# A four-layer graph network kernel: VectorE's own semaphore instructions replaced by waits for tile releases, with a new order of the steps

## The chip, the cores and the metric

The kernel runs on one core of a Trainium2 chip. Its time is the device time of one execution in microseconds (us), the median of three runs. A core has five engines with queues of their own: TensorE (PE), VectorE (DVE), ScalarE (ACT), GpSimd (POOL) and SyncE (SP, which issues the DMAs). They meet only through semaphores.

## The reference

`x` is 32 batches of 512 nodes with 128 features, `adj` one 512x512 adjacency matrix of ones and zeros. Four graph layers follow each other, each on the normalised input and added to it:

```python
h = jnp.maximum(_layernorm(x, axis=-1), 0.0)
x = x + _L0_gnn_ref(h, adj, ...)   # attention with pair indices, softmax over rows, plus h @ self_weight
h = jnp.maximum(_layernorm(x, axis=-1), 0.0)
x = x + _L1_gnn_ref(h, adj, ...)   # attention, layernorm, aggregation, two-layer MLP
h = jnp.maximum(_layernorm(x, axis=-1), 0.0)
x = x + _L2_gnn_ref(h, adj, ...)   # attention, elu
h = jnp.maximum(_layernorm(x, axis=-1), 0.0)
x = x + _L3_gnn_ref(h, adj, ...)   # out = softmaxed edge weights: diagonal @ h0 + rest @ h1 + bias
```

Layers 1 and 2 hold the attention that matters here: `e = leaky_relu(s_i + t_j)`, masked by `adj`, softmax over j, times the features.

## The kernel before, in words

The 32 batches are worked in 16 groups of two. A group has 1024 rows, which lie as 8 tiles of 128 rows by 128 features in SBUF. Six groups are under way at a time, each in a slot `s` with its own buffers (`X[s]` the residual, `Y[s]`, `HE[s]`, `HT[s]` the transposed rows, `HI[s]`/`LOW[s]` a value split in two parts, `CE[s]`, `MX[s]` small coefficients); so group 13 is in slot 1, groups 14 and 15 in slots 2 and 3, group 11 in slot 5.

A group passes through 56 steps, listed in `STEPS` with the engines that take part. The suffix is the layer. For layers 1 and 2: `stat` (DVE's `bn_stats`, POOL's reciprocal root), `scale` (ACT writes the normalised rows), `norm` (PE transposes them, ACT copies with relu), `feat` (features times weights; DVE copies two score columns out and takes their maximum), `top` (PE spreads the maximum, DVE makes exponents, ACT takes the exponentials), `weigh`, `spreada`/`spreadb` (PE spreads one score per batch over a tile), `atta`/`attb` (DVE makes the attention matrix `PT`, four instructions of 128x512, L1307; PE multiplies it with the features, 16 matmuls), then `collect`/`gat`/`gin`/`mlp` in layer 1 and `elu2a`, `elu2b`, `elu2` in layer 2. Layer 0 has `coef0`, `cmax0`, `coefb0` (narrow matmuls of 4 columns, `wcols` and `CS`), `split0`, `agg0`, `self0`; layer 3 has `feat3` (`W3`, 256 columns) and `agg3` (48 matmuls on `a3_hi` and `a3_lo`). `PREP` is a seventeenth list, work done once on the edge weights.

The order in which an engine takes the steps is written out by hand: in `TURNS`, one digit per step says from which group (0 to 9, a to f; g is `PREP`) the next step comes. Each engine has its string, and within a group the steps keep their order. Nothing is decided at run time: an engine whose next step is not ready stands still.

PSUM is cut into 8 banks of 128x512. `HOMES` gives the bank of each tile in PE's order. Each bank has two semaphores, `psum_full` (PE has written) and `psum_taken` (the reader has read; PE may write again). PE asks with `turned(...)` or `open_tile(...)`, a reader asks with `filled(...)` and raises `taken` on its last instruction. `read_by_act(...)` on DVE waits for a tile's release, here that of DVE's own instruction, and so until DVE has finished it. Only two `PT` buffers exist (`RING`).

The steps that the change touches, on DVE: `split0` (L1227 on) scales a tile pair twice, into `YF` and `VA`; `attend` (L1296 on) makes `PT`; `elud2` (L1345 on) is `elu2a` and `elu2b`; `agg3` (L1466 on) adds the last result to `X`. At the end of each DVE waits until it has finished and then raises a semaphore with an instruction of its own:

```python
a.then_inc(p_full[r], 1)
dve.wait_ge(p_full[r], u.matrix(name)[1] + 1)
dve.sem_inc(read, 1)
```

That is the end of `attend`. Of the raises, `scaled` is waited for by ACT's `split0`, `read` (the release of the spread tile) by PE's later tile in that bank, `gated` by ACT's `elu2` and `result` by SP's `store`.

Of the kernel before, what the change touches and what calls it, by code (L numbers as in the profile page):

```python
# [41 lines left out]
RING = 2  # L42
# [78 lines left out]
    "pe": ("gggg0110101020g2120012413240303410101033114040511522553305120232123223032304143130550100001110404151"  # L121
           "4214515042454505252101321322624224226736676743472662373343234433643474684867688646786758757383757785"
           "84838848854595599599655a6a99a56a6a79799699669769657a56656a777787a78776b6ab8abb8aa67b78aab8b889798ba8"
           "bacb8cbb8c9b9dadadbc8c89dd9899ca9aaaca99ade9aecaccdeeccbcedbdcdeedb9dbdde9e9bebeebbcbecefbfffafbbcdf"
           "cfdaafffdffdfcfccceccdecddcfdfeddedffbdeeefefeffebeecffdcffbdcedfefef"),
    "act": ("g0110g2021g01244303011200341105501103015142021303221023021351033012001014114250542403105245402215314"
           "512243563222446372573644622372343473346443688668747668537537655638847748854788599755596aa9686a659798"
           "76699a76956765957997776a87ab866b6788baa77878baaa889ab9b8caac9bbd98ada8cbb898d9cab99a9adaabeeccc9cbed"
           "dcabe9cddbbce9ded9bcbeebbbcdfecfaedfacfcbdedaffdfdfcceffcdcecdeffecfdfdedffbbeedffeeefffbcdcedfcdefe"
           "fef"),  # L130
    "dve": ("g102gggg1010g0g0204131120001112234504032110330411041520352201313355422022331330045241134555000101200"
           "2414001145151412553042230451615422372242262627667633446652737673233434834764438677866484388674785788"
           "6736585783884987455799a9595956a99a98566a55799a99a6866775966a596aa77b667787767ab7ab988a6abbbc7ba8bb8a"
           "a7988bdab8cb8b889d9caabdcc8d9dc89bca9eacd9cad9aa9becca9ddce9ceeebddceeeddbabd9cae9ecbebfebdcffbffdbb"
           "fbefccffadeaffffddebcfcccefcfcdcdfdededffcddeedffeebeeffeffefcfddcbefef"),
    "pool": ("01201043120153240135234010521430510021421562374626234736847783865384547989a596a96755a679ab67687b87bc"
           "ab98da89c8adbcae9cdde9ebc9ebdabfcfafefdcdfcebfdefcdbecfdefef"),
    "sp": ("403510617228394a5b6c7d8e9fadcbef"),
}
HOMES = ("0123456701234567012347056123412341235641702356415670415067125304304356717204356072071241207431256074"  # L140
         "3612543612354072361546150723461341634613461507234615072346150723461613450726712345016273473273250164"
         "7324732432473501647235021364721364507213607452136260745264051372640513762517640325031725031371250303"
         "0643071625642565307615423073067306713540276540465270413040410310652743103146527652703140314652703146"
         "5270314652462574031640235702135647021356024756024756060612437506750567124376105246105246371052463716"
         "3710524367105721045367210721074503764076354542154207163546356435643543207165436543652407316247357325"
# [20 lines left out]
def gnn_kernel(nc, x, adj, Wo_d, Ws_d, att0_d, Wp_d, bp_d, asrc_d, adst_d, gatg_d, gatb_d, eps_d, W1_d, b1_d,  # L166
# [12 lines left out]
    with ctx:  # L179
# [74 lines left out]
        class Step:  # L254
# [18 lines left out]
            def matrix(self, name):  # L273

                m = mat_at[name, self.group]
                before = mat_of[m - RING] if m >= RING else None
                return m % RING, m // RING, before
# [382 lines left out]
        with nc.Block() as block:  # L660
# [483 lines left out]
            def _(dve):  # L1144
# [200 lines left out]
                def elud2(u, s, b):  # L1345
# [14 lines left out]
                    for h in range(2):  # L1360
                        read_by_act(u, "att2" + "ab"[b], s, h)
# [163 lines left out]
```

## Time and profile before

| | us |
|---|---|
| median of three runs | 1015.85 |
| lowest and highest run | 1012.22, 1019.29 |
| profiled execution, span from first to last instruction | 1013.8 |
| PE busy | 949.6 |
| DVE busy | 859.2 |
| ACT busy | 632.5 |
| POOL busy | 555.4 |

The page gives no other time of the profiled execution than its span. Busy is the time in which at least one instruction of the engine runs. Matmuls overlap each other, and their ends are modelled. Waits and instructions that only raise a semaphore are not counted as busy. "Idle before <- X" names who released the instruction that the engine waited with.

### The profile page before, as it was taken

Reading aid. Unit: us, or ns where it says so; the run is one execution under the profiler, and the core shown is the slowest. Engines: PE = TensorE matmul, PEld = TensorE weight load, DVE = VectorE, ACT = ScalarE, POOL = GpSimd, SP = SyncE. Lnnn points to the kernel's source line nnn. Section 1 sums busy time; section 2 is a strip of 40 time slices with the busy share of each in tenths; the row PEclk is TensorE's granted clock in tenths of the full one; section 3 lists DMA queues with packets and bytes.
Section 4 is the critical chain, followed back from the end, with each engine's and each line's share of the span. In section 5 each row is a group of like instructions: output and inputs, shape, how many; then the busy total and the mean of one; then the engine's idle time right before and its main releaser. Section 6 shows DMA issues by size and latency. Waiting matters only on the chain. (4 is left out here: it accounts for less than half of the span.)

```text
span 1013.8 us, 21212 instructions
## 1 busy us (share of the span) xinstructions
PE 949.6 (94%) x7355; PEld 902.1 (89%) x7355; DVE 859.2 (85%) x2526; ACT 632.5 (62%) x1655; POOL 555.4 (55%) x1171
## 2 busy tenths in 40 slices
PE   5989999999999999999999999998999999997998
PEld 4779998988998889899989899998999898886897
DVE  5988897989979988977888888799988989779874
ACT  3347547686668653775686664877548584677741
POOL 3535264582575652765566565654636744467850
PEclk9978999999999999999999999999999999999999
DMA  5020000000020010011000101101000100000003
GB/s 135 1 63 1 1 2 1 2 1 1 2 83 2 1 43 2 1 37 49 2 1 2 43 1 43 43 2 33 11 1 2 42 2 2 21 1 2 1 1 105
DMA packets 38071, 19.99 MB, mean 20 GB/s; under 512 B 3142, under 2 KB 37452, under 8 KB 37964
## 3 DMA queue, kind: packets, MB, share of 16 engines
q1 hardware_dynamic: 36080, 18.42, 6.5%
q8 instruction: 59, 0.97, 0.4%
q10 hardware_dynamic: 1884, 0.21, 0.2%
q14 instruction: 48, 0.39, 0.1%
HBM read 10.23 MB, written 8.39 MB: 18 GB/s over the span
## 5 line engine op out<-in xcount | busy, mean ns | idle before, releaser
L686 PE MATMUL ps<-HE,PT 128*128 128x129 f32 x2048 | 238.5, 276 | 3.2 <-issue 1.9
L686 PEld LDWEIGHTS ps<-HE,PT 128*128 128x128 f32 x2048 | 233.1, 192 | 5.4 <-issue 4.8
L451 ACT ACTIVATE Y<-X,SM 128x128 f32<-128x128 f32 x512 | 204.0, 491 | 49.3 <-POOL SM L447 49.1
L1307 DVE SCALAR_TENSOR_TENSOR PT<-ps,CE,maskT 128x512 f32<-128x512 f32 x256 | 174.2, 742 | 19.2 <-PE ps L810 11.8
L432 POOL TENSOR_TENSOR SM<-ST 128x8 f32<-128x8 f32 x96 | 29.5, 307 | 269.4 <-DVE ST L1170 269.3
L443 POOL TENSOR_TENSOR SM<-SM,minus_half 128x8 f32<-128x8 f32 x96 | 163.3, 1701 | 7.6
L686 PE MATMUL ps<-W,HT 128*128 128x128 f32 (+1 forms) x768 | 126.1, 311 | 0.0
L686 PEld LDWEIGHTS ps<-W,HT 128*128 128x128 f32 x768 | 115.6, 193 | 8.9
L1170 DVE BATCH_NORM_STATS2 ST<-X 128x6 f32<-128x128 f32 x512 | 104.8, 278 | 3.1 <-DMA X<-in_x_dram 0.4
L703 PE MATMUL ps<-ident,Y 128*128 128x128 f32 x640 | 85.6, 278 | 10.7 <-ACT Y L451 10.2
L703 PEld LDWEIGHTS ps<-ident,Y 128*128 128x128 f32 x640 | 72.2, 143 | 16.3 <-ACT Y L451 14.4
L958 ACT ACTIVATE HT<-ps 128x512 f32<-128x512 f32 x96 | 51.9, 597 | 37.8 <-PE ps L703 37.6
L686 PE MATMUL ps<-HI,a_hi 128*128 128x256 f32 x256 | 73.2, 286 | 1.6 <-DVE LOW L1460 1.4
L686 PE MATMUL ps<-HI,a_lo 128*128 128x256 f32 x256 | 72.0, 281 | 0.0
L686 PE MATMUL ps<-LOW,a_hi 128*128 128x256 f32 x256 | 72.0, 281 | 0.0
L996 ACT ACTIVATE HE<-ps,HE 128x128 f32<-128x128 f32 x256 | 69.2, 382 | 0.0
L451 ACT ACTIVATE HE<-Y,SM 128x128 f32<-128x128 f32 x128 | 51.1, 495 | 27.1 <-POOL SM L447 27.0
L686 PE MATMUL ps<-gin_hi,LOW 128*128 128x512 f32 x128 | 57.8, 451 | 2.5 <-DVE X L1251 1.6
L451 ACT ACTIVATE Y<-Y,SM 128x128 f32<-128x128 f32 x128 | 51.0, 491 | 12.0 <-POOL SM L447 12.0
L1170 DVE BATCH_NORM_STATS2 ST<-Y 128x6 f32<-128x128 f32 x256 | 51.8, 275 | 6.2 <-ACT Y L1025 5.3
L1116 POOL TENSOR_TENSOR LOWB<-HE,HIB 128x1024 fp32r<-128x1024 f32 x16 | 37.6, 2351 | 30.3 <-ACT HIB L979 30.3
L686 PEld LDWEIGHTS ps<-HI,a_hi 128*128 128x128 f32 x256 | 48.5, 189 | 2.5 <-DVE LOW L1460 2.0
(260 smaller groups left out, 2335.6 us busy)
## 6 DMA issues: line engine op xcount, KB each, us to landing
X<-in_x_dram SPq DMA_DIRECT2D x32, 256.0 KB, 3.5
out_dram<-X SPq DMA_DIRECT2D x32, 256.0 KB, 2.8
adj_raw<-in_adj_dram SPq DMA_DIRECT2D x4, 256.0 KB, 3.5
W<-in_L_gnn_W_dram SPq DMA_DIRECT2D x2, 64.0 KB, 3.8
W<-in_L_gnn_W_dram SPq DMA_DIRECT2D x1, 128.0 KB, 3.6
bias<-in_L_gnn_bias_dram SPq DMA_DIRECT2D x2, 64.0 KB, 4.1
Wo<-L_gnn_others_weight_dram ACTq DMA_DIRECT2D x1, 64.0 KB, 3.1
feat1w<-in_L_gnn_Wp_dram ACTq DMA_DIRECT2D x1, 64.0 KB, 3.5
```

The source lines that it names most:

```text
L432: TT(sm[:, S_DIF, :], st[:, :, 1], st[:, :, 4], ALU.subtract)
L443: link(TT(sm[:, S_RSTD, :], sm[:, S_VAR, :], minus_half[:], ALU.pow))
L451: a = nc.scalar.activation(dst[:, n, 0:F], src[:, n, 0:F], func, scale=SM[s][:, S_RSTD, n:n + 1], bias=SM[s][:, S_SHIFT, n:n + 1])
L686: return nc.tensor.matmul(o, w, m, start=start, stop=stop, skip_group_check=True)
L703: mm = T_(o[:, t * P:(t + 1) * P], Y[s][:, t * G + b, 0:F], ident[:])
L958: a = A(HT[s][:, b, :], o, ACT.Relu)
L996: a = A(HE[s][:, k, 0:F], o[:, 2 * P * b:2 * P * b + F], ACT.Identity, scale=HE[s][:, k, F:F + 1])
L1116: TT(LOB[s], VA[s], HIB[:].bitcast(F32), ALU.subtract).then_inc(sig["by_pool"][s], 1)
L1170: a = V.bn_stats(ST[s][:, n, :], src(n))
L1307: a = V.scalar_tensor_tensor(out=PT[r][:, j, :], in0=o, scalar=CE[s][:, c:c + 1], in1=maskT[:, j, :].bitcast(F32), op0=ALU.max, op1=ALU.mult)
```

## The change

Three semaphores go (`matrix_full`, `result`, and half the use of `scaled`, with a third of the use of `gated`). DVE no longer waits for itself and no longer raises them; who needed them waits for the `taken` releases of the tiles that DVE's last instructions read. With that `TURNS` and `HOMES` are other strings.

```diff
 TURNS = {
-    "pe": ("gggg0110101020g2120012413240303410101033114040511522553305120232123223032304143130550100001110404151"
...
+    "pe": ("gggg01011200201g100221313240030410041013314041252513132052025521243143232013031535040003100110104511"
...
 HOMES = (...)
@@ SP, store
-                    sp.wait_ge(sig["result"][s], count(u.g, 1, 0))
+                    for h in range(2):
+                        slot, k = u.tile("agg3", h)
+                        sp.wait_ge(taken[slot], k + 2)
@@ PE, attend
-                    r, k, _ = u.matrix(name)
+                    r = u.matrix(name)[0]
                     turned(u, "feat" + name[3], s, T - 1)
-                    pe.wait_ge(p_full[r], k + 1)
+                    turned(u, "spread" + name[3:], s, 0)
@@ ACT, split0
-                    act.wait_ge(sig["scaled"][s], count(u.g, 2, 1))
+                    for h in range(2):
+                        slot, k = u.tile("feat0", h)
+                        act.wait_ge(taken[slot], k + 2)
@@ ACT, elu2
-                    act.wait_ge(sig["gated"][s], count(u.g, 3, 2))
+                    for name in ("att2a", "att2b"):
+                        for h in range(2):
+                            slot, k = u.tile(name, h)
+                            act.wait_ge(taken[slot], k + 2)
@@ DVE, split0
-                        read_by_act(u, "feat0", s, h)
-                    dve.sem_inc(sig["scaled"][s], 1)
@@ DVE, attend
-                    a.then_inc(p_full[r], 1)
-                    dve.wait_ge(p_full[r], u.matrix(name)[1] + 1)
-                    dve.sem_inc(read, 1)
+                    a.then_inc(read, 1)
@@ DVE, elud2
-                    for h in range(2):
-                        read_by_act(u, "att2" + "ab"[b], s, h)
-                    dve.sem_inc(sig["gated"][s], 1)
@@ DVE, agg3
-                        read_by_act(u, "agg3", s, h)
-                    dve.sem_inc(sig["result"][s], 1)
```

SP's string goes from "403510617228394a5b6c7d8e9fadcbef" to "345020611728394a5b6c7d8e9fabcdef".

DVE, the attend steps of group 7 in layer 2 (`CE1` is its slot, `PT0` and `PT1` the two matrices; the bracket gives the semaphores an instruction waits for). Before:

```order
L1170 BN_STATS ST0<-X0 128x6 [waits dve_order]
L1170 BN_STATS ST0<-X0 128x6 x7
L1307 SCALAR_TENSOR_TENSOR PT0<-ps3,CE1,maskT 128x512 [waits psum_full6,dexp_1]
L1307 SCALAR_TENSOR_TENSOR PT0<-ps3,CE1,maskT 128x512 x3
L1307 SCALAR_TENSOR_TENSOR PT1<-ps0,CE1,maskT 128x512 [waits matrix_full0,psum_full1,psum_full2,dexp_1]
L1307 SCALAR_TENSOR_TENSOR PT1<-ps0,CE1,maskT 128x512 x3
L1170 BN_STATS ST2<-Y2 128x6 [waits matrix_full1,psum_taken5,psum_taken0]
L1170 BN_STATS ST2<-Y2 128x6 x7
```

The same place now:

```order
L1176 BN_STATS ST0<-X0 128x6 [waits dve_order]
L1176 BN_STATS ST0<-X0 128x6 x7
L1311 SCALAR_TENSOR_TENSOR PT0<-ps3,CE1,maskT 128x512 [waits psum_full7,psum_full6,dexp_1]
L1311 SCALAR_TENSOR_TENSOR PT0<-ps3,CE1,maskT 128x512 x3
L1176 BN_STATS ST2<-Y2 128x6 [waits psum_taken6,psum_taken0]
L1176 BN_STATS ST2<-Y2 128x6 x7
L1311 SCALAR_TENSOR_TENSOR PT1<-ps0,CE1,maskT 128x512 [waits psum_full1,dexp_1]
L1311 SCALAR_TENSOR_TENSOR PT1<-ps0,CE1,maskT 128x512 x3
```

The wait for `matrix_full0` ahead of the second matrix is gone, and the statistics of group 8 (`ST2<-Y2`) have moved from behind the second attend step to between the two.

PE near the end. `Y3` and `W2,HT3` belong to group 15, `Y5` to group 11, `HE1,PT1` to group 13. Before:

```order
L703 MATMUL ps3<-ident,Y3 128x128 x4
L703 MATMUL ps0<-ident,Y3 128x128 x4
L686 MATMUL ps0<-bias_2,pick 128x512
L686 MATMUL ps0<-W2,HT3 128x128 x4
L686 MATMUL ps2<-bias_2,pick 128x512
L686 MATMUL ps2<-W2,HT3 128x128 x4
L703 MATMUL ps1<-ident,Y5 128x128 x8
L686 MATMUL ps3<-HE1,PT1 128x129 x8
```

Now:

```order
L704 MATMUL ps3<-ident,Y3 128x128 x8
L704 MATMUL ps0<-ident,Y5 128x128 x4
L704 MATMUL ps2<-ident,Y5 128x128 x4
L687 MATMUL ps1<-bias_2,pick 128x512
L687 MATMUL ps1<-W2,HT3 128x128 x4
L687 MATMUL ps0<-bias_2,pick 128x512
L687 MATMUL ps0<-W2,HT3 128x128 x4
L687 MATMUL ps3<-HE1,PT1 128x129 x16
```

Group 11's transposes (`Y5`) have moved from behind group 15's W2 matmuls to a place between its transposes and these matmuls.

PE a little later: `Y3` and `feat2w,HT3` belong to group 15, `MX2` and `CE2` to group 14, `W3,HT5` is feat3 of group 11. Before:

```order
L686 MATMUL ps3<-feat2w,HS2 128x128 x2
L703 MATMUL ps2<-ident,Y3 128x128 x4
L703 MATMUL ps0<-ident,Y3 128x128 x4
L801 MATMUL ps3<-ident,MX2 128x128 x2
L686 MATMUL ps2<-feat2w,HT3 128x130 x2
L686 MATMUL ps0<-feat2w,HT3 128x130 x2
L686 MATMUL ps3<-feat2w,HT3 128x130 x4
L810 MATMUL ps0<-ident,CE2 128x128 x4
L686 MATMUL ps2<-feat2w,HS3 128x128 x2
L801 MATMUL ps1<-ident,MX3 128x128 x2
L810 MATMUL ps1<-ident,CE2 128x128 x4
L686 MATMUL ps2<-W3,HT5 128x256 x2
```

Now:

```order
L687 MATMUL ps1<-feat2w,HS2 128x128 x2
L802 MATMUL ps3<-ident,MX2 128x128 x2
L687 MATMUL ps0<-W3,HT5 128x256 x2
L687 MATMUL ps2<-W3,HT5 128x256 x2
L687 MATMUL ps1<-W3,HT5 128x256 x2
L687 MATMUL ps3<-W3,HT5 128x256 x2
L704 MATMUL ps0<-ident,Y3 128x128 x4
L704 MATMUL ps2<-ident,Y3 128x128 x4
L811 MATMUL ps0<-ident,CE2 128x128 x4
L811 MATMUL ps1<-ident,CE2 128x128 x4
L687 MATMUL ps2<-feat2w,HT3 128x130 x2
```

All of group 11's feat3 has moved ahead of group 15's transposes, and both spreads of group 14 (`CE2`) stand between these and the feat2w matmuls.

PE near the start, with the narrow matmuls `CS` and `wcols0` of layer 0 (the number behind `HT` is the slot, here also the group). Before:

```order
L703 MATMUL ps3<-ident,Y3 128x128 x8
L686 MATMUL ps0<-CS2,adj_top 128x4 x8
L686 MATMUL ps2<-wcols0,HT4 128x4 x8
L703 MATMUL ps0<-ident,Y0 128x128 x4
L703 MATMUL ps2<-ident,Y0 128x128 x4
L686 MATMUL ps0<-wcols0,HT3 128x4 x8
L686 MATMUL ps3<-bias_p,pick 128x2x130
L686 MATMUL ps3<-feat1w,HT0 128x130 x2
L686 MATMUL ps3<-bias_p,pick 128x2x130
L686 MATMUL ps3<-feat1w,HT0 128x130 x2
```

Now:

```order
L687 MATMUL ps2<-wcols0,HT3 128x4 x8
L687 MATMUL ps0<-CS2,adj_top 128x4 x8
L704 MATMUL ps2<-ident,Y4 128x128 x4
L704 MATMUL ps0<-ident,Y4 128x128 x4
L704 MATMUL ps1<-ident,Y0 128x128 x4
L704 MATMUL ps3<-ident,Y0 128x128 x4
L687 MATMUL ps2<-bias_p,pick 128x2x130
L687 MATMUL ps2<-feat1w,HT0 128x130 x2
L687 MATMUL ps0<-bias_p,pick 128x2x130
L687 MATMUL ps0<-feat1w,HT0 128x130 x2
```

One of the two wcols blocks has moved away to a later place, and the other stands ahead of `CS2`.

## Rows read from the trace of the kernel before

**Rows 1.** The page's first part: busy us, share of the span, instructions.

```profile
PE 949.6 (94%) x7355; PEld 902.1 (89%) x7355; DVE 859.2 (85%) x2526; ACT 632.5 (62%) x1655; POOL 555.4 (55%) x1171
```

**Rows 2.** Stretches: length, PE, PEld, DVE, ACT, POOL busy (instructions), PE clock, DMA, GB/s.

```profile
25.00:100.00 75.00, 68.04 (x420) 62.96 (x419) 65.26 (x199) 39.52 (x92) 36.85 (x84) 0.82 0.08 22
100.00:900.00 800.00, 769.29 (x6128) 734.47 (x6127) 694.99 (x2034) 522.94 (x1380) 449.08 (x972) 0.99 0.05 15
900.00:950.00 50.00, 40.28 (x298) 36.23 (x298) 41.38 (x124) 37.26 (x105) 34.50 (x70) 1.00 0.00 1
950.00:1000.00 50.00, 50.00 (x381) 48.33 (x381) 39.90 (x108) 23.14 (x55) 25.91 (x28) 1.00 0.12 33
90.00:105.00 15.00, 14.21 (x85) 13.88 (x83) 10.61 (x49) 9.53 (x23) 6.27 (x20) 0.66 0.01 2
```

**Rows 3.** Waits (us in total, times, longest), and the shares of the chain.

```profile
POOL SM L432 <- DVE ST L1170: 269.3, 55, 20.7
...
DVE X L1472 <- PE ps L686: 24.9, 14, 5.1
...
PE ps L703 <- ACT Y L451: 10.2, 16, 2.6
...
PE 14%; DVE 7%; ACT 2%; POOL 2%; issue 1%; DVEq 0%
```

**Rows 4.** Timeline of DVE: start us, us, instruction, count [idle before <- releaser].

```profile
774.13 1.65 DVE L1170 BATCH_NORM_STATS2 ST<-X 128x6 f32<-128x128 f32 x8
775.69 2.71 DVE L1307 SCALAR_TENSOR_TENSOR PT<-ps,CE,maskT 128x512 f32<-128x512 f32 x4
778.64 2.73 DVE L1307 SCALAR_TENSOR_TENSOR PT<-ps,CE,maskT 128x512 f32<-128x512 f32 x4 [0.24 <-DVE PT L1307]
781.52 1.41 DVE L1338 SCALAR_TENSOR_TENSOR Y<-HE,ps 128x512 f32<-128x512 f32 x2 [0.15 <-DVE PT L1307]
782.97 1.23 DVE L1342 SCALAR_TENSOR_TENSOR X<-Y,X 128x1024 f32<-128x1024 f32 x1
...
955.94 0.16 DVE L1352 TENSOR_SCALAR SM<-ps 128x2 f32<-128x2 f32 x1 [0.20 <-issue]
...
992.69 1.41 DVE L1472 TENSOR_TENSOR X<-X,ps 128x512 f32<-128x512 f32 x2 [0.24 <-DVE X L1472]
```

**Rows 5.** The chain that ended last, in order of time: start us, us, what.

```profile
775.77 2.64 DVE PT L1307 x4
...
920.15 2.74 DVE PT L1307 x4
...
984.31 5.65 PE ps L686 x48
989.96 0.87 PE ps L703 x8
```

**Rows 6.** Timeline of PE from 920 to 950.

```profile
922.70 0.47 PE L686 MATMUL ps<-bias,pick 128*128 128x512 f32 x1 [1.15 <-ACT HT L954]
...
925.72 1.09 PE L703 MATMUL ps<-ident,Y 128*128 128x128 f32 x8 [0.54 <-ACT Y L451]
...
932.95 1.09 PE L703 MATMUL ps<-ident,Y 128*128 128x128 f32 x8 [2.56 <-ACT Y L451]
...
938.98 1.09 PE L703 MATMUL ps<-ident,Y 128*128 128x128 f32 x8 [1.50 <-ACT Y L451]
...
941.03 2.02 PE L686 MATMUL ps<-feat2w,HT 128*128 128x130 f32 x16 [0.75 <-ACT HT L956]
...
944.51 3.69 PE L686 MATMUL ps<-W,HT 128*128 128x256 f32 x16
948.03 7.31 PE L686 MATMUL ps<-HE,PT 128*128 128x129 f32 x64
```

**Rows 7.** Timeline of ACT, group 15's last normalised rows.

```profile
983.41 3.19 ACT L451 ACTIVATE Y<-X,SM 128x128 f32<-128x128 f32 x8 [1.92 <-POOL SM L447]
```

**Rows 8.** Timeline of PE near the start.

```profile
95.33 3.41 PE L686 MATMUL ps<-wcols,HT 128*128 128x4 f32 x16
```

More of the change, by code:

```diff
@@ L120 @@
 TURNS = {
-    "pe": ("gggg0110101020g2120012413240303410101033114040511522553305120232123223032304143130550100001110404151"
[L122 to L135, printed above, removed]
@@ new lines @@
+    "act": ("g02101g210g01334200410130240115053012102104150223113510322014323004100031125115442025502410325140521"
+            "342135342226436472764346227233457343344468683667548758636775353868747545848796895587596a968a8665a979"
+            "6996756a9566975797776a78a789b6b88667aba877b8aa79aa98bc8ab8ac9bd8bd9ba8ba8c8d9b9caa999adaaebecc9debdc"
+            "c9cbecaddb9b9ceebdcbedefcbfcdbbeaeffcdcbdadfafdefdfccebfccfdcdefdfdecfefedffeebdefbefefffceddcfcdeef"
+            "fef"),
+    "pool": ("02110031402135420231350415420150310210214563274626237463784783586384547959a8969a657a5967a7b686b87b7a"
+             "bc89da889cbdacaed9cde99ebcebfdbafcafefdcbdcfedfbefcedfcdefef"),
@@ L276, in matrix @@
                 before = mat_of[m - RING] if m >= RING else None
-                return m % RING, m // RING, before
+                return m % RING, before
         def walk(e, run):
@@ L292, in gnn_kernel @@
         taken = [sem(f"psum_taken{i}") for i in range(BANKS)]
-        p_full = [sem(f"matrix_full{i}") for i in range(RING)]
         sig = {n: [sem(f"{n}_{s}") for s in range(NS)] for n in (
-            "result", "stored", "var", "rstd", "normed", "extent", "scaled", "hi", "lo", "range", "dexp", "by_act",
+            "stored", "var", "rstd", "normed", "extent", "scaled", "hi", "lo", "range", "dexp", "by_act",
             "by_pool", "gated")}
@@ L971, in split0 @@
                 def split0(u, s):
-                    act.wait_ge(sig["scaled"][s], count(u.g, 2, 0))
+                    act.wait_ge(sig["scaled"][s], count(u.g, 1, 0))
                     A(HI[s][:], YF[s], ACT.Copy).then_inc(sig["hi"][s], 1)
-                    act.wait_ge(sig["scaled"][s], count(u.g, 2, 1))
+                    for h in range(2):
+                        slot, k = u.tile("feat0", h)
+                        act.wait_ge(taken[slot], k + 2)
                     if u.group > 0:
@@ L1013, in gatl1 @@
                 def gatl1(u, s):
-                    act.wait_ge(sig["gated"][s], count(u.g, 3, 0))
+                    act.wait_ge(sig["gated"][s], count(u.g, 1, 0))
                     A(HI[s][:], VA[s], ACT.Relu).then_inc(sig["hi"][s], 1)
@@ L1299, in attend @@
                     dve.wait_ge(sig["dexp"][s], count(u.g, 4, 2 * n + 1))
-                    r, k, before = u.matrix(name)
+                    r, before = u.matrix(name)
                     if before is not None:
```

31 lines of the change are left out of this document (19 added, 12 removed).

## The prediction

> **What bounds the kernel now.** I read the page's busy times first [rows 1]. TensorE (PE) is busy 949.6 us of 1013.8 (94%), VectorE (DVE) 859.2 (85%), ScalarE (ACT) 62%, GpSimd (POOL) 55%. So nearly all time is TensorE's own work, and a change that removes no matmul can gain only what TensorE waits, 1013.8-949.6 = 64.2 us, and what it loses at the lower clock.
>
> Then the table of stretches, for where these lie [rows 2]. TensorE is without work for 75-68.04 = 7.0 us between 25 and 100, 800-769.29 = 30.7 between 100 and 900, 50-40.28 = 9.7 between 900 and 950, none up to 1000. These are 47.4; the other 16.8 are the loads of the first 25 us and the last addition and store, out of this change's reach. The granted clock is 0.82 of 2.4 GHz between 25 and 100 and 0.66 between 90 and 105: there TensorE runs partly at 1.2 GHz.
>
> A wait shorter than a matmul's record hides inside "busy". The weight-load columns show it better: 48.33 of 50 us where nothing waits (950 to 1000), so 1.67/50 = 3.3% are their own gaps. Between 100 and 900 they are idle 800-734.47 = 65.5 us; less 3.3% of 800 (27) leaves 39 us, against the 30.7 above. That is the ceiling for the middle.
>
> Next, who makes TensorE wait [rows 3]: most of all the transposes for ScalarE's normalised rows, 10.2 us in 16 waits. Behind ScalarE stand GpSimd's statistics, and GpSimd waits 269.3 us for DVE's BATCH_NORM_STATS2. The chain that ended last is 14% PE, 7% DVE, 2% ACT, 2% POOL of the span [rows 3], 27% in all, so it reaches back some 270 us, and in 71 of these DVE sets the pace. DVE counts as a source of latency, not by its share.
>
> **The removed waits, part by part.** DVE ends a step thus: it waits until its own last instruction has finished, then raises a semaphore with an instruction of its own. The timeline gives the price [rows 4]. With no wait between them the next record begins before the last ends: the statistics begin at 774.13 and last 1.65, to 775.78, and PT begins at 775.69, so -0.09. Behind a wait alone it is 781.52+1.41 = 782.93 to 782.97, 0.04. Behind wait and raise it is 775.69+2.71 = 778.40 to 778.64, 0.24, and 778.64+2.73 = 781.37 to 781.52, 0.15. So an attend step gives back 0.24 to 0.33, say 0.28: 4 per group, 16 groups, 64 x 0.28 = 18 us. An elu2 half: the gap of 0.20 ahead of 955.94 and the lost overlap, 0.29, x32 = 9.3 us. agg3: 0.24 ahead of 992.69 and the overlap, 0.33, and 0.13 for the wait inside the pair (0.04+0.09), 0.46 x16 = 7.4 us. split0 has the same form, a pair with a wait inside and a raise behind, another 7.4 us at most. Sum 42 us of DVE's time, 4% of the span.
>
> How much reaches the end? Only what lies on the chain that TensorE waits for. In the chain's last 270 us I count 8 attend steps that are followed by a DVE piece, from 775.77 to 920.15 [rows 5]: 8 x 0.28 = 2.3 us. Over the 914 us from 100 us on that is x3.4, 7.6 us. But each such saving runs into TensorE's own queue, which is mostly full; I take two thirds, **-5 us**. Bounds: 0 (TensorE's own work covers all) and -39 (the ceiling above).
>
> One rule speaks against this term. The Trainium skill, "VectorE: DVE Perf Modes", section "The DRAIN you can't avoid", says that chaining VectorE operations without semaphores gains nothing: eight copies with one behind each took as long as eight with one behind the last. By it the term would be 0. This case's trace shows another thing, 0.24 us against -0.09 [rows 4]; the page's case has increments on completion, and here a wait and an instruction stand between.
>
> New waits: TensorE's attend waits for the release of the spread tile in place of the matrix semaphore; both are raised by the fourth PT instruction or right behind it, so it starts no later. ScalarE's split0 and elu2 wait for two and four releases, the last of which comes 0.1 to 0.2 us before the old raise. The store on SP waits for two releases; behind it in SP's queue stands only the load into the same slot, which needs the store anyway. These cost nothing, and if one did, it would be the 0.03 to 0.04 us of a wait.
>
> **The new order at the end.** Between 920 and 945 us TensorE waits 1.15, 0.54, 2.56, 1.50 and 0.75 us [rows 6]. In the new order the transposes of group 11 (Y5) stand between those of group 15 (Y3) and its W2 matmuls: their 0.9 us fill most of the 1.15, and their own wait of 0.54 goes, as their ScalarE step has moved ahead: 1.4 us. Group 11's feat3 (W3,HT5, from 944.51 to 948.03, 3.5 us) now stands ahead of the transposes that waited 1.50. That wait goes; from these transposes to the feat2w matmuls ScalarE needs 941.03-938.98 = 2.05 us, in which the transposes (0.9) and now two spreads (0.9) stand, so of the 0.75 some 0.25 stay: 2.0 us, from which I take 0.1 for a DVE step that now comes later. Together **-3.3 us**. The 2.56 stays, as DVE's work ahead of it is the same. Bounds 0 and -9.7 (all waits of the stretch).
>
> Is something late after that? Group 15's last transposes began at 989.96 [rows 5]; ScalarE had the rows ready at 983.41+3.19 = 986.6 [rows 7], 3.4 us sooner. Between group 15's last attention and these there stood three agg3 and one feat3, now two and two: 5.65 us [rows 5] less and 3.5 more, cover is 2.2 us less, and 1.2 stay. Nothing late; if it were, 1 to 2 us.
>
> **The new order at the start.** Between 90 and 105 the clock is 0.66 [rows 2], within narrow matmuls (4 columns) and transposes; 16 wcols records take 3.41 us there [rows 8]. CS, wcols, 8 transposes and wcols stood in a row. Now there is one wcols ahead of CS, then 16 transposes, then feat1 (130 columns), and the other wcols comes later. The stretch lost (1-0.66) x 15 = 5.1 us. I take half, **-2.5 us**; bounds -5 and +5 (a stretch twice as long).
>
> **The middle.** All other places are reshuffled too. Counted in matmuls, the distances between a step and the one that needs it are about as they were, some wider, some closer; I take 0, with bounds of +-8 (a quarter of 30.7).
>
> **Sum.** On the profiled execution, of which the page gives the span: 1013.8-5-3.3-2.5 = 1003.0. The median of the runs is 1015.85, 2.05 above it; 1003.0+2.05 = **1005 us**, 1.1% less than before. About 1% is what a measurement of this kernel tells from no change, so "same" is 1005.7 to 1026.0.
>
> **Rivals.**
> A, the freed DVE time is swallowed: TensorE's work hides it, or DVE waits for its inputs instead (it waits 24.9 us for agg3's matmuls alone [rows 3]). For it: TensorE at 94% [rows 1]; against: DVE's 71 us in the chain. Then only the order's 5.8 count: 1015.85-5.8 = 1010. The rule of the Trainium skill quoted above would lead to the same time.
> B, slower: DVE takes its steps strictly in turn, and an old group's agg3, feat3 or elu2 directly ahead of a young group's attend step makes the young one wait for the old one's matmuls. By the written order there were 4 such places, now 6 (agg3 3, now 4). The longest wait of agg3 is 5.1 us, the mean 24.9/14 = 1.8 [rows 3]; it decides from about 2 us, when TensorE has nothing else in front of the attention. Two more waits of 5.1, and one more stretch at the lower clock like the one that cost 5, with no gain elsewhere: 1015.85+10.2+5 = 1031. Against: the mean wait is short.
> C, more than forecast: the hidden waits of the middle (39 us) shrink by a third, 13 instead of 5: 1005-8 = 997 or less.
>
> **Chances.** Forecast 0.55 (own range 998 to 1012; 0.36 of it below 1005.7, 0.19 above), A 0.26, B 0.10, C 0.09. Faster 0.36+0.09 = 0.45, same 0.19+0.26 = 0.45, slower 0.10. The range takes in most of C, the forecast and A, and reaches towards B: 993 to 1019.
>
> **What would show it.** Right: behind PT a DVE gap of at most 0.05 us, or an overlap; DVE's busy time the same and its idle time less; TensorE's idle time from 900 to 950 near 6 us; the clock between 90 and 105 above 0.8; TensorE's idle time from 100 to 900 near 26. Wrong: if the middle's idle time is 31 or more, if the lower clock has come at other places, or if DVE waits longer for agg3's matmuls ahead of PT.

## The result, and the profile after

The changed kernel takes 1009.9 us (median of 14 runs, 1008.1 to 1011.8) against 1013.6 us for the kernel before, run beside it (14 runs, 1012.2 to 1019.3). The ratio is 0.9957, with a 95% interval from 0.9941 to 0.9973: 0.4% faster, where 1.1% was forecast. 1005 was predicted, so the forecast lies 5 us too low. The saving itself was forecast at 10.8 us and came out at 4: the forecast started from 1015.85 us, 2.3 above the 1013.6 that the kernel before takes in 14 runs, and this happened to bring it nearer. What it is wrong about besides is where the gain comes from.

The page's busy line, which answers to [rows 1]; the span is 1007.7 us:

```profile
PE 943.0 (94%) x7355; PEld 901.4 (89%) x7355; DVE 866.1 (86%) x2526; ACT 632.5 (63%) x1655; POOL 566.6 (56%) x1171
```

The table of stretches, which answers to [rows 2] (columns: busy us of PE, of its weight loads, of DVE, ACT and POOL, then granted clock, DMA share, GB/s):

```profile
25.00:100.00 75.00, 64.59 (x390) 60.10 (x389) 64.29 (x190) 34.26 (x80) 32.43 (x82) 0.82 0.08 22
100.00:900.00 800.00, 769.99 (x6181) 740.06 (x6180) 707.75 (x2056) 532.39 (x1404) 467.22 (x980) 0.99 0.05 15
900.00:950.00 50.00, 42.82 (x329) 39.14 (x329) 42.46 (x131) 32.21 (x90) 35.69 (x64) 1.00 0.00 1
90.00:105.00 15.00, 14.27 (x110) 13.88 (x108) 12.68 (x52) 11.61 (x29) 9.05 (x27) 0.89 0.00 1
75.00:90.00 15.00, 13.33 (x93) 13.14 (x93) 14.65 (x40) 5.20 (x10) 10.36 (x20) 0.81 0.23 60
```

The same 15 us from 75 on in the kernel before:

```profile
75.00:90.00 15.00, 14.70 (x126) 14.51 (x126) 14.33 (x42) 9.67 (x22) 12.06 (x27) 0.99 0.00 1
```

So the lower clock has moved rather than gone: from 0.66 to 0.89 between 90 and 105, and from 0.99 to 0.81 between 75 and 90.

TensorE's visible waits are no shorter in sum: 1007.7-943.0 = 64.7 us, before 64.2. The weight-load column gives a first idea of where the time went. Its idle time between 100 and 900 is 59.9 us, before 65.5; between 900 and 950 it is 10.9, before 13.8; but between 25 and 100 it is 14.9, before 12.0.

Such a comparison has two weaknesses: the two kernels do different work in the same microseconds, and a load that runs at the lower clock counts as busy for longer, so lost time looks like work. I therefore also compared the same amount of work. For each kind of matmul I took its usual distance to the next one (the same price for all kernels, the 35th percentile of the distances in four of the traces), added these up along each trace, and read how long each kernel takes for the first 11% of the sum, the next 77% and the last 12%. e1 to e3 are runs of the next section. One profiled execution stands behind each row; with a lower or higher percentile no entry moves by more than 0.5 us. The 14 to 15 us of the span that are missing lie ahead of the first matmul and behind the last.

| us | first 11% | next 77% | last 12% |
|---|---|---|---|
| before | 128.3 | 748.8 | 122.7 |
| changed | 132.0 | 742.8 | 119.0 |
| e1, removed waits alone | 124.1 | 746.0 | 122.7 |
| e2, new order alone | 134.2 | 763.9 | 120.4 |
| e3, changed with one step moved | 125.9 | 742.7 | 119.0 |

The changed kernel gains 6.0 us in the middle and 3.7 at the end, and loses 3.7 at the start.

DVE's gap behind `PT` is gone. Its timeline after, the answer to 0.24 and 0.15 in [rows 4]:

```profile
911.64 2.71 DVE L1311 SCALAR_TENSOR_TENSOR PT<-ps,CE,maskT 128x512 f32<-128x512 f32 x4
914.27 1.40 DVE L1340 SCALAR_TENSOR_TENSOR Y<-HE,ps 128x512 f32<-128x512 f32 x2
```

911.64+2.71 = 914.35, and the next record begins at 914.27, 0.08 sooner. This is so at 56 of the 64 attend steps (mean -0.08); at the other eight the next instruction waited for another engine.

The start has a new wait. TensorE's timeline:

```profile
66.54 2.16 PE L893 MATMUL ps<-ident,v 128*128 128x128 f32 x16
68.89 1.02 PE L687 MATMUL ps<-CS,adj_top 128*128 128x4 f32 x8 [0.19 <-DVE a_lo L1446]
74.51 0.58 PE L687 MATMUL ps<-HI,maskT 128*128 128x256 f32 x1 [4.59 <-DVE LOW L1247]
```

agg0 of group 0 begins at 74.51, before at 70.76, and TensorE waits 4.59 us for DVE's `LOW`. DVE and ACT take their half of `eturn` (L893) ahead of group 0's `split0`, and TensorE now does `eturn` behind feat0 of group 1. ScalarE stands still for it, and VectorE for ScalarE's `a_hi`:

```profile
67.43 2.06 ACT L1060 ACTIVATE a_hi<-ps 128x512 fp32r<-128x512 f32 x4 [8.30 <-PE ps L893]
```

```profile
68.06 2.48 DVE L1446 TENSOR_TENSOR a_lo<-ps,a_hi 128x512 fp32r<-128x512 f32 x4 [2.26 <-ACT a_hi L1060]
```

At the end, TensorE's timeline, which answers to [rows 6]:

```profile
919.10 1.97 PE L704 MATMUL ps<-ident,Y 128*128 128x128 f32 x16 [1.82 <-ACT Y L450]
921.34 0.47 PE L687 MATMUL ps<-bias,pick 128*128 128x512 f32 x1 [0.27 <-issue]
...
929.24 2.02 PE L687 MATMUL ps<-feat2w,HT 128*128 128x130 f32 x16 [0.97 <-ACT HT L957]
...
936.56 1.29 PE L704 MATMUL ps<-ident,Y 128*128 128x128 f32 x8 [0.95 <-DVE X L1462]
```

The 2.56 us ahead of transposes is gone, and what is left are waits of 1.82, 0.97 and 0.95. The last one is of a new kind: TensorE waits until DVE has read a tile of feat3 (`X`), as feat3 now stands ahead. In all TensorE is idle 7.2 of 50 us here, before 9.7.

The waits in sum, TensorE's two largest of the main part and DVE's two largest (columns: us in total, times, longest), which answer to [rows 3]:

```profile
PE ps L704 <- ACT Y L450: 11.0, 7, 2.3
...
PE ps L687 <- DVE LOW L1247: 6.3, 2, 4.6
```

```profile
DVE X L1471 <- PE ps L687: 22.6, 13, 2.8
DVE PT L1311 <- PE ps L811: 13.0, 11, 5.8
```

TensorE waits for ScalarE's rows as long as before in sum, seven times instead of sixteen. DVE waits a little less for agg3's matmuls (22.6 against 24.9 us), and a little more for the spreads ahead of `PT` (13.0 us in 11 waits, the longest 5.8; before 11.8 in 9, the longest 3.4).

One number was in no term of the forecast: DVE is busy 866.1 us, before 859.2, with the same instructions. What lies behind it is in the last section.

### The profile page after: what moved, and what is told of

Read it like the earlier page. It is cut to its first block and busy times, and to the rows that moved or that the text cites. A ratio compares the mean times of both kernels' runs of the same rounds, so it can differ in the third digit from the quotient of the medians.

```text
span 1007.7 us, 21096 instructions
## 1 busy us (share of the span) xinstructions
PE 943.0 (94%) x7355; PEld 901.4 (89%) x7355; DVE 866.1 (86%) x2526; ACT 632.5 (63%) x1655; POOL 566.6 (56%) x1171
## 5 line engine op out<-in xcount | busy, mean ns | idle before, releaser
L687 PE MATMUL ps<-W,HT 128*128 128x128 f32 (+1 forms) x768 | 125.9, 312 | 0.0
L704 PEld LDWEIGHTS ps<-ident,Y 128*128 128x128 f32 x640 | 74.5, 146 | 16.8 <-ACT Y L450 14.1
L687 PE MATMUL ps<-gin_hi,HI 128*128 128x512 f32 x128 | 50.4, 394 | 0.0
```

The source lines that it names most:

```text
L687: return nc.tensor.matmul(o, w, m, start=start, stop=stop, skip_group_check=True)
L704: mm = T_(o[:, t * P:(t + 1) * P], Y[s][:, t * G + b, 0:F], ident[:])
```

## The experiments

Four theories were open. A saving in us below is a difference of two ratios times the time of the kernel before, about 1015 us. T1, additive: the removed waits and the new order each give their share. T2: the order gives nothing and the waits everything. T3: the waits give nothing and the order everything, rival A of the prediction. T4: the two need each other, since an order is laid out for one pace of VectorE.

**e1, the waits alone.** The changed code with the `TURNS` and `HOMES` of before.

> The waits and raises removed, the order of before. Theory W (the removed waits make the gain, the order only went along): ratio to before 0.994 to 0.997, about as the whole change (0.9957). Theory O (the new order makes it, DVE's freed time is swallowed by the fixed old order): 0.999 to 1.001. Under both the gap behind PT on DVE is gone, and DVE has some 16 us more idle time.

Measured: ratio 0.9957 [0.9939, 0.9975], the same number as the whole change. The page:

```profile
PE 949.1 (94%) x7355; PEld 903.4 (90%) x7355; DVE 848.9 (84%) x2526; ACT 631.7 (63%) x1655; POOL 554.2 (55%) x1171
```

So the removed waits give 4.4 us in the old order, and T3 falls. The expected 16 us more of idle time on DVE did not come: it is 1007.5-848.9 = 158.6 us, before 154.6, since busy time and span shrank too.

What did the removal free on DVE? The prediction priced it at 42 us. The traces give less: the gaps behind the 160 places that lost a wait sum to 56.8 us before and 31.2 in e1, 25.6 less; in the new order they sum to 52.9 in e2 and 24.5 in the changed kernel, 28.4 less (an overlap counts as negative). In the old order attend freed 12.4 of the 18 us that it was priced at, elu2 6.0 of 9.3, agg3 3.1 and split0 4.0 of 7.4 each: at some of these places DVE waits for another engine anyway, and the price per place was too high for the last two.

Two stretches of e1:

```profile
100.00:900.00 800.00, 772.65 (x6152) 738.36 (x6151) 690.27 (x2037) 527.09 (x1390) 455.01 (x980) 0.99 0.05 15
900.00:950.00 50.00, 42.69 (x313) 39.77 (x313) 41.41 (x127) 37.86 (x108) 35.47 (x58) 0.93 0.00 1
```

The weight loads idle 61.6 and 10.2 us there, before 65.5 and 13.8. At the end TensorE waits less with no step moved, as its timeline shows:

```profile
913.27 1.09 PE L704 MATMUL ps<-ident,Y 128*128 128x128 f32 x8 [0.84 <-ACT Y L450]
915.51 0.47 PE L687 MATMUL ps<-bias,pick 128*128 128x512 f32 x1 [1.15 <-ACT HT L955]
...
924.29 1.09 PE L704 MATMUL ps<-ident,Y 128*128 128x128 f32 x8 [0.23 <-ACT Y L450]
...
931.01 1.09 PE L704 MATMUL ps<-ident,Y 128*128 128x128 f32 x8 [2.20 <-ACT Y L450]
...
933.07 3.68 PE L687 MATMUL ps<-feat2w,HT 128*128 128x130 f32 x16 [0.75 <-ACT HT L957]
```

The third wait is the 2.56 us of before, now 0.23; the 1.50 has grown to 2.20, and the 0.54 is gone. In sum TensorE waits 7.3 us in the last 12% of the work, before 10.0. No step was moved, and the other two kernels below that have the old order without attend's waits show the same (e5 7.7, e13 7.4), so it is the removed waits that did this. But this execution won no time by it: the granted clock between 900 and 950 is 0.93, before 1.00, and the feat2w matmuls of the last line take 3.68 us, before 2.02. The table has 122.7 us for both.

**e2, the order alone.** Before's code with the new `TURNS` and `HOMES`.

> The new order with the old waits and raises. Theory O: ratio 0.994 to 0.997. Theory W: 0.999 to 1.002. A third theory (each is fitted to the other: the new order is only good with the waits gone): above 1.002, while the waits alone are at 1.000.

Measured: 1.0156 [1.0131, 1.0182], 16 us slower than before. This is the finding of the study: on the old code the new order loses. From 1.0156 to 0.9957 the removed waits are worth 2.0 points in the new order, and 0.43 in the old. T1 and T2 fall, T4 is left (in its expectation it had the removed waits alone at 1.000, which they are not). The page and the stretch from 100 to 900:

```profile
PE 958.9 (93%) x7355; PEld 914.4 (89%) x7355; DVE 876.0 (85%) x2526; ACT 633.0 (61%) x1655; POOL 565.8 (55%) x1171
```

```profile
100.00:900.00 800.00, 761.43 (x6009) 729.77 (x6008) 697.31 (x2014) 517.49 (x1362) 456.27 (x962) 0.98 0.05 15
```

The profiled execution is the slowest of the six; its span is 19.1 us longer. 12.3 of these are weight loads that take longer (914.4-902.1): the mean granted clock is 0.967, before 0.980, with stretches at the lower level in more places. The other 6.8 are loads waiting. By the table 15.1 us are lost in the middle (8.7 of these as waits of TensorE, 37.9 against 29.2) and 5.9 at the start, and 2.3 are won at the end. The gaps and the lower clock came together here; that the one brought the other was not tested.

**e3, one place of the start.** The changed kernel with TensorE's `eturn` ahead of feat0 of group 1:

```diff
-    "pe": ("gggg01011200201g100221313240030410041013314041252513132052025521243143232013031535040003100110104511"
+    "pe": ("gggg0101120020g1100221313240030410041013314041252513132052025521243143232013031535040003100110104511"
...
-HOMES = ("0123456710234567102345671203645024502714365027127504127502741361436150274674361530263704204372047620"
+HOMES = ("0123456710234567102345671204502364502714365027127504127502741361436150274674361530263704204372047620"
```

> The changed kernel, with eturn ahead of feat0 of group 1 in TensorE's order. Theory S (the new wait of 4.6 us of TensorE for LOW near 70 us, together with the later start, took back some 3 us of what the rest gained): agg0 of group 0 begins 2 to 3 us sooner, and the ratio to before is 0.992 to 0.994, 2 to 3 us less than the whole change. Rival: the lost time is made up by later waits anyway, since ScalarE and DVE are equally behind: ratio as the whole change, 0.9957.

Measured: 0.9920 [0.9902, 0.9938], 3.7 us faster than the changed kernel and faster than either kernel of the case. agg0 of group 0 begins 1.8 us sooner (2 to 3 were expected):

```profile
72.71 0.39 PE L687 MATMUL ps<-HI,maskT 128*128 128x256 f32 x1 [2.75 <-DVE LOW L1247]
```

**e4, attend's wait and raise put back.** The changed kernel, and in `attend`:

```diff
-                    a.then_inc(read, 1)
+                    a.then_inc(p_full[r], 1)
+                    dve.wait_ge(p_full[r], u.matrix(name)[1] + 1)
+                    dve.sem_inc(read, 1)
```

> The changed kernel with wait and raise back in the attend steps alone (64 of the 128 places, 18 of the 42 us of DVE's time by the prediction's prices). If the time scales with DVE's freed time: the loss is 18/42 of what the waits are worth in the new order, which is the difference of e2 and the whole change. If the attend steps are the ones on the chain: nearly all of it. If none is on it: ratio 0.9957.

Measured: 1.0062 [1.0043, 1.0080]. Of the 2.0 points that the four parts give in the new order attend alone gives 1.05. That is its share by time as the traces have it: the gaps behind the attend steps are 15.8 us in e2 and -0.3 in the changed kernel, 16.1 of the 28.4 us. The expectation's 18 of 42 was too small a share.

**e5, attend's wait and raise removed, old order.** Before, and in `attend` of DVE and of TensorE:

```diff
-                    a.then_inc(p_full[r], 1)
-                    dve.wait_ge(p_full[r], u.matrix(name)[1] + 1)
-                    dve.sem_inc(read, 1)
+                    a.then_inc(read, 1)
...
-                    pe.wait_ge(p_full[r], k + 1)
+                    turned(u, "spread" + name[3:], s, 0)
```

> Before's code and order, with the wait and the raise taken out of attend alone (64 of them, 18 of the 42 us of VectorE time that all four parts free). So far the four parts together gave 0.43% in the old order and 2.0% in the new one, and attend alone 1.05% in the new one. Theory 1, the old order has little use for VectorE time wherever it is freed: attend gives its share by time, 18/42 of 0.43%, ratio 0.998. Rival, attend is the part that TensorE waits for at once and the rest is covered: ratio 0.9957, the same as all four. Second rival, attend's time is covered and the end parts (agg3, elu2) gave everything: 1.000.

Measured: 0.9971 [0.9955, 0.9986]. In the old order attend gives 0.3 points, a third of what it gives in the new. The interval leaves both shares of the 0.43 open, by time or all of it; only nothing is excluded.

**e6, a wait without the raise.** The changed kernel, behind attend's last instruction:

```diff
+                    read_by_act(u, "spread" + name[3:], s)
```

> The changed kernel, with a wait of VectorE for its own attend instruction put back (64 times), but no raise behind it. Wait and raise together cost 1.0151/0.9957... in one number 10.7 us (ratio 1.0062 against 0.9957). Before's gaps behind attend were 0.15 to 0.24 us against an overlap of 0.08 to 0.09 without them. Theory: the wait lets the instruction drain (about 0.15 to 0.2 us of the 0.28) and carries some 60% of the loss: ratio 1.002. Rival, the raise carries it: ratio 0.996. Second rival, the wait carries all: 1.006.

Measured: 1.0020 [0.9996, 1.0044], 0.6 points of the 1.05.

**e7, a raise without a wait.** The changed kernel, at the same place:

```diff
+                    dve.sem_inc(spare, 1)
```

> The changed kernel, with a raise of a semaphore that nobody waits for put behind each attend instruction (64 times), and no wait. Theory: a raise alone is issued while the instruction ahead of it still runs, costs under 0.1 us, and gives some 0.2 to 0.4%: ratio 0.999. Rival, a raise is what empties the engine: ratio near 1.006. Second rival, it costs nothing: 0.996.

Measured: 0.9977 [0.9964, 0.9990]; its interval overlaps that of the changed kernel. So it isn't told from nothing; its middle value is 2 us. DVE's timeline, first of e6, then of e7:

```profile
774.48 2.72 DVE L1311 SCALAR_TENSOR_TENSOR PT<-ps,CE,maskT 128x512 f32<-128x512 f32 x4
777.23 0.69 DVE L1268 TENSOR_TENSOR X<-X,ps 128x512 f32<-128x512 f32 x1
```

```profile
773.77 2.72 DVE L1312 SCALAR_TENSOR_TENSOR PT<-ps,CE,maskT 128x512 f32<-128x512 f32 x4
776.40 0.68 DVE L1269 TENSOR_TENSOR X<-X,ps 128x512 f32<-128x512 f32 x1
```

A wait alone: 777.20 to 777.23, a gap of 0.03. A raise alone: 776.49 to 776.40, an overlap of 0.09, as with nothing. The same at 58 places of e6 (mean 0.03) and at 56 of e7 (mean -0.08). Both together: 0.18, the mean of 60 places in e4. So the wait costs 0.11 us against the overlap, a raise no gap by itself, and a raise behind a wait 0.15 more. Why it does so only behind a wait was not tested. Over 64 places these are 7 and 17 us of DVE's time, and they cost 6.4 and 10.7 us of the kernel's, with intervals of 2 to 3 us to either side: in the new order most of it shows.

**e9, VectorE slower in the old order.** Before, and behind each attend step:

```diff
+                    for _ in range(2):
+                        link(V.memset(spare[:], 0.0))
```

> Before, with two memsets of one element behind each attend instruction (64 times), each waiting for the one ahead of it: VectorE's queue is held some 0.4 us longer at each attend, about 26 us in all; nothing is computed with them. It asks whether an order is flat only on the side on which VectorE gets faster. Theory, each order is laid out for a pace of VectorE, and being slower than that pace costs about 0.5 us of time for each us of VectorE (the slope that attend's wait shows in the new order): 13 us, ratio 1.013. Rival, the old order has slack of VectorE on both sides and its slope stays at 0.1: 2.6 us, ratio 1.003.

Measured: 1.0154 [1.0137, 1.0171], 15.6 us. DVE's timeline shows that less was added than planned:

```profile
785.70 2.71 DVE L1308 SCALAR_TENSOR_TENSOR PT<-ps,CE,maskT 128x512 f32<-128x512 f32 x4
788.59 0.18 DVE L1314 MEMSET spare<- 128x1 f32 x2 [0.18 <-DVE PT L1308]
788.86 2.73 DVE L1308 SCALAR_TENSOR_TENSOR PT<-ps,CE,maskT 128x512 f32<-128x512 f32 x4
```

From the end of `PT` to the next one it is 788.86-788.41 = 0.45, before 0.24: 0.21 more, 64 times 13.4 us (26 were planned). So 13.4 us more cost 15.6, while in e1 25.6 us less gave 4.4. The old order is steep on the slow side and, for these places, much flatter on the other, as if it had been laid out for the pace that VectorE had.

**e12, VectorE faster than the new order's layout.** The changed kernel without the first line of `gat1`'s pair; the multiplication by `gat_g` is left out of the computation.

```diff
-                    link(V.tensor_tensor(VA[s], VA[s], repeat(gat_g[:], TG), ALU.mult))
```

> The changed kernel without the multiplication by gat_g in gat1 (that part of the computation is left out): 16 VectorE instructions of 1.32 us each and the wait behind them, 22 us of VectorE time less than the new order was laid out for. Theory: an order is steep where VectorE is slower than its layout and flat where it is faster (the old order: +15.6 us for 14 us more, -4.4 us for 42 us less; the new order: +20 us for 42 us more), so here some 0.1 us per us: 2 us, ratio 0.9935. Rival, the new order simply needs VectorE more than the old one, on both sides: 0.5 us per us, 11 us, ratio 0.985.

Measured: 0.9867 [0.9839, 0.9896], 9 us less for 22 us of DVE. The rival was right: the new order isn't flat on its fast side. Here T4 is too simple.

**e13, the same cut in the old order.** e1 with the edit of e12.

> e1 (the removed waits, with the order of before) without the multiplication by gat_g in gat1 (that part of the computation is left out), 16 VectorE instructions and the wait behind each, about 22 us of VectorE time. In the new order the same cut gave 0.9 points (ratio 0.9867 against 0.9957). The old order made only 4.4 us of the 42 us that the waits had freed. Theory 1, the old order has slack of VectorE and is flat whatever is cut: ratio 0.994 to 0.9935 (2 us). Rival 2, what counts is where the cut lies: gat1 stands on the path of its group (ScalarE and TensorE wait for it) in either order, and the cut gives as much as in the new one: ratio 0.987. Between them, 0.990, neither is told.

Measured: 0.9899 [0.9877, 0.9922], 6 us less than e1, between the two expectations. The page of e12, then that of e13:

```profile
PE 942.3 (94%) x7355; PEld 902.4 (90%) x7355; DVE 844.6 (84%) x2510; ACT 633.3 (63%) x1655; POOL 557.0 (56%) x1171
```

```profile
PE 945.4 (94%) x7355; PEld 900.2 (90%) x7355; DVE 831.5 (83%) x2510; ACT 631.7 (63%) x1655; POOL 544.2 (54%) x1171
```

DVE's busy time fell by 866.1-844.6 = 21.5 us in the new order and by 848.9-831.5 = 17.4 in the old. Each us cut here gives 9.1/21.5 = 0.42 in the new and 5.9/17.4 = 0.34 in the old; each us freed by the removed waits gave 20.2/28.4 = 0.71 in the new and 4.4/25.6 = 0.17 in the old. So the old order is not flat either; at most for the waits at their places, and with intervals of 2 to 3 us on the 4.4 and the 5.9 even that is not certain. The intervals of e12 and e13 overlap, so for this cut the two orders aren't told apart.

**e11, the first groups in turn.** e3, and the first steps (`stat0`, `scale0`) of group 1 ahead of group 2's:

```diff
-    "dve": ("g021gggg1010g02g001314010012113220503401401231340232210351034351221054524125433423001153500250012130"
+    "dve": ("g012gggg1010g02g001314010012113220503401401231340232210351034351221054524125433423001153500250012130"
...
-    "act": ("g02101g210g01334200410130240115053012102104150223113510322014323004100031125115442025502410325140521"
+    "act": ("g01201g210g01334200410130240115053012102104150223113510322014323004100031125115442025502410325140521"
...
-    "pool": ("02110031402135420231350415420150310210214563274626237463784783586384547959a8969a657a5967a7b686b87b7a"
+    "pool": ("01210031402135420231350415420150310210214563274626237463784783586384547959a8969a657a5967a7b686b87b7a"
```

> e3 (eturn ahead of feat0 of group 1), and besides the statistics of group 1 ahead of those of group 2 on VectorE, POOL and ScalarE, as in the order of before. In e3 TensorE waits 2.07 us at 47.40 for ScalarE's scaling of group 1, in before 0.49. Theory: the wait shrinks by some 1.6 us, and half of it comes back at the idle spots behind it (0.96 and 2.75 us): ratio 0.991 (e3: 0.992). Rival, group 2's data then come later to coef0 and all is given back: 0.992. Second rival: the whole 1.6 us: 0.9905. What five rounds can tell is some 2 us, so this is a try for a better kernel rather than a test.

Measured: 0.9929 [0.9903, 0.9954], not told apart from e3. The 2.07 us moved to the next step:

```profile
47.80 6.31 PE L687 MATMUL ps<-wcols,HT 128*128 128x4 f32 x32 [2.80 <-ACT HT L959]
```

**e8, a probe for the long DVE records.** The changed kernel with this behind its last work; POOL's part runs beside DVE's:

```diff
+                for _ in range(5):
+                    link(TT(LOB[0], HIB[:].bitcast(F32), HIB[:].bitcast(F32), ALU.subtract))
...
+                for _ in range(6):
+                    for n in range(2):
+                        V.bn_stats(ST[1][:, n, :], X[1][:, n, :])
+                    link(V.reciprocal(SM[1][:, S_INV, :], SM[1][:, S_INV, :]))
+                    V.tensor_tensor(YF[1][:, 0:4, :], area[0].rearrange("p (r f) -> p r f", f=F),
+                                    bcast(SM[1][:, S_B, 0:4], F), ALU.mult)
+                    link(V.tensor_tensor(SM[1][:, S_Q, :], SM[1][:, S_B, :], SM[1][:, S_INV, :], ALU.mult))
```

> The changed kernel with a probe behind its last work: POOL does five subtractions of 128x1024 floats from SBUF to SBUF, and beside them VectorE does six rounds of: two bn_stats and a reciprocal (one tensor from SBUF each), a multiplication of a PSUM tile by a column (one tensor from SBUF, one from PSUM) and a multiplication of two 128x8 tensors of SBUF. In the main part an instruction of 128x8 with two tensors from SBUF took 2.16 us beside a POOL instruction of 2.18 us, where it otherwise takes 0.17. Theory: only instructions with two tensors from SBUF are held until POOL's instruction ends: the small multiplication shows 1 to 2 us in about five of six rounds, and the others show 0.28, 0.20 and 0.68 us as always. Rival, everything that VectorE reads from SBUF is slowed beside POOL: bn_stats and the reciprocal are longer too. Second rival, the long record was chance: all six small ones show 0.17. The time tells nothing here: 10 to 15 us are added at the end.

Measured: the theory's five of six, each 0.7 us long where 1 to 2 were expected. Its rows stand in the last section.

## Why the prediction was right in its range and wrong in its steps

**The removed waits, -5 us: right in size, in the old order.** e1 measured -4.4. The duration behind attend stands too: 0.28 us per step against 0.27 (means of 0.19 before and -0.08 after). The total of 42 us does not: the traces show 25.6 and 28.4. The rule of the Trainium skill, "VectorE: DVE Perf Modes", section "The DRAIN you can't avoid", would have made this 0; the measurements decide against it for this pattern. A wait costs 0.11 us and wait with raise 0.26 (e6, e4), while an increment on completion or a raise alone leaves the overlap as it was (e7). The page says of its copies only that a semaphore stood behind each; I read that as an increment on completion. The -5 itself came out well by luck: the 7.6 us under it counted attend steps alone, the two thirds were a guess, and attend alone gives 0.29 points or 2.9 us in the old order (e5). In the new order the same removal is worth 20 us.

**The order at the end, -3.3 us: the size came, the step that failed is "the 2.56 stays, as DVE's work ahead of it is the same".** The end is 3.7 us shorter, but e1 has the same fall of TensorE's waits with no step moved: 7.3 us in the last 12% of the work and 7.2 in the changed kernel, before 10.0. DVE's work was the same, and it was done sooner. That e1's end is still 122.7 us is the lower clock of this one execution. In the two other traces of the old order with attend's waits gone and no such fall of the clock (e5, e13) the end takes 120.0 and 119.4 us, in the new order 119.0. So the moved steps gave some 1 us at most beyond what the waits had given, and 2.3 with the old waits (e2).

**The order at the start, -2.5 us: wrong in sign.** The clock between 90 and 105 rose to 0.89 as forecast, but between 75 and 90 it fell from 0.99 to 0.81, so the stretch from 25 to 100 stayed at 0.82 as a whole. The start costs 3.7 us more than before, and 7.9 more than in e1. I had looked only at the narrow matmuls, and not at what stands ahead of agg0 of group 0: `eturn`, moved on TensorE past feat0 of group 1, holds DVE's and ACT's queues. It costs 3.7 us by the medians, and in e3's trace the first 11% of the work takes 6.1 us less than in the changed kernel's.

**The middle, 0 us: the term that should not have stood by itself.** I summed it as if the order had one value whatever the code. By the table the new order costs 15.1 us in the middle with the old code (e2 against before) and gains 3.2 with the new (the changed kernel against e1), each from one pair of executions. That the whole change measures the same as e1 is thus no sign that the order does nothing there: in these traces the start takes back what middle and end give. "Distances counted in matmuls are about as they were" says nothing of how far they suffice at one pace of VectorE and not at another.

So the sum 1013.8-5-3.3-2.5 is too low by an order term of 5.8 us that, with the waits gone, measures 0. The range held the result because it was wide enough for rival A too. Rival A named the time that came, 1010, and for the opposite reason: it let the order alone count. Its own claim, that the freed DVE time is swallowed, holds of the old order for five sixths of 25.6 us, and not of the new one. Rival B, a young group behind an old one on DVE, did not show at agg3: DVE waits 22.6 us for its matmuls, before 24.9 [rows 3], the longest 2.8 instead of 5.1. One slip in the working changes little: the chain's shares [rows 3] sum to 26%, not 27.

Of the signs that I named, the gap behind `PT` and TensorE's time from 900 to 950 came (7.2 us idle; near 6 was said). DVE's busy time should have stayed and rose by 7; the middle should have had 26 us idle and has 30.0, just under the 31 that I had called wrong. One sign of being wrong did come: the lower clock at another place, between 75 and 90.

What stays open: which steps make the new order so steep at before's pace; no run moved single steps in the middle. The order with `eturn` mended (e3) has a ratio 0.4 points below e1's; by the table, one execution each, it gains 3.3 us in the middle and 3.7 at the end and loses 1.8 at the start, and what it gains at the end is for the most part the fall of the clock in e1's execution.

## What to carry to other kernels

Where every engine takes its steps in a written order, the order and the instructions have one value together, not two that can be added. Measure code and order apart, both ways round (here -0.4% and +1.6%, together -0.4%), before either is called a gain; and after an instruction has become cheaper the old order may still be as good as a new one.

On VectorE a wait for its own last instruction cost 0.11 us here, and 0.26 with an instruction that raises a semaphore behind it; let the last instruction raise it on completion. Compare kernels of different order at the same amount of work, and look at the granted clock beside it: in the same microseconds they do different things. When a step is moved on one engine, look at every engine that shares it: `eturn` cost 3.7 us through two other queues.

## What the runs showed of the hardware that was not expected

Some of DVE's instructions are held while POOL works on large tensors. The same code has DVE busy 848.9 us in the old order (e1) and 866.1 in the new; before and e2 stand 859.2 to 876.0, again 17 us apart. One place in the changed kernel, DVE's timeline and POOL's:

```profile
73.23 1.23 DVE L1247 TENSOR_TENSOR LOW<-Y,HI 128x1024 fp32r<-128x1024 f32 x1
74.37 0.17 DVE L1222 TENSOR_REDUCE SM<-ps 128x8 f32<-128x16 f32 x1
74.57 2.16 DVE L1225 TENSOR_TENSOR SM<-SM,CE 128x8 f32<-128x8 f32 x1
76.77 0.17 DVE L1226 SCALAR_TENSOR_TENSOR SM<-SM 128x8 f32<-128x8 f32 x1
```

```profile
74.53 2.18 POOL L1122 TENSOR_TENSOR LOWB<-HE,HIB 128x1024 fp32r<-128x1024 f32 x1 [12.50 <-ACT HIB L982]
```

An instruction of 8 columns that has two tensors in SBUF takes 2.16 us where it otherwise takes 0.17, and ends with POOL's, at 76.73 and 76.71. The probe (e8) has this five times in a row, DVE's timeline of its second and last rounds, and POOL's:

```profile
1006.76 0.49 DVE L1501 BATCH_NORM_STATS2 ST<-X 128x6 f32<-128x128 f32 x2
1007.16 0.18 DVE L1502 RECIPROCAL SM<-SM 128x8 f32<-128x8 f32 x1
1007.38 0.69 DVE L1503 TENSOR_TENSOR Y<-ps,SM 128x512 f32<-128x512 f32 x1
1007.99 0.71 DVE L1505 TENSOR_TENSOR SM<-SM 128x8 f32<-128x8 f32 x1
...
1015.88 0.16 DVE L1505 TENSOR_TENSOR SM<-SM 128x8 f32<-128x8 f32 x1
```

```profile
1004.81 9.78 POOL L1151 TENSOR_TENSOR LOWB<-HIB 128x1024 fp32r<-128x1024 f32 x5 [19.66 <-DVEq L1498]
```

POOL's second subtraction ends at about 1004.81+2x1.96 = 1008.7, and so does DVE's small one (1007.99+0.71). Statistics, reciprocal and the PSUM operand are not touched. When POOL is done, at 1014.6, the small one takes 0.16. The Trainium skill states it ("GPSIMD Engine Reference", section "Specifications", the row on SBUF interfaces: VectorE instructions with two SBUF inputs contend with GpSimd), and the trace agrees. It is a cost that an order carries and that no list of durations shows: moving a step on either engine can put a 2 us hold on an 8-column instruction.

Does this make up the 17 us? Count the DVE records that are over 0.15 us longer than the median of their kind. In e1 there are 10, with 12.8 us too much in all; in the changed kernel 24, with 31.1 us. The difference, 18.3 us, is the 17, and each of these records runs beside an instruction of POOL. But only 16 of the 24 (18.2 us) have two tensors as inputs, which is the form that was probed. The other 8 (12.9 us) are `TENSOR_SCALAR` instructions of 4 or 8 columns, with one tensor in SBUF and single values; each ends 0.03 us behind the end of a POOL instruction, as the held instructions of 8 columns do (0.02 to 0.03). One of them, and POOL's beside it:

```profile
467.60 2.50 DVE L1297 TENSOR_SCALAR CF<-DS,MX 128x4 f32<-128x4 f32 x2
```

```profile
467.74 2.35 POOL L1131 TENSOR_TENSOR HT<-HT,bias 128x1024 f32<-128x1024 f32 x1
```

So POOL holds this form too by all that the trace shows, but no probe had it. What the 17 us cost in time was not tried.
